# Attention and expert layer on one core: one more row block normalised on VectorE, row ranks and two routing steps placed earlier, and new instruction orders

## The reference

```python
xn = _layernorm(x, axis=-1)
x = x + _L0_attn_ref(xn, Wq, Wk, Wv, Wo) + _L0_ffn_ref(xn, ...)
# attention: 32 query heads of 128 in 8 groups, 8 key heads, causal
q = q * cos + _rotate_half(q) * sin
k = k * cos + _rotate_half(k) * sin
scores = jnp.einsum('bkgtd,bksd->bkgts', qg, k) * scale
attn = jax.nn.softmax(jnp.where(causal, scores, -jnp.inf), axis=-1)
out = jnp.einsum('bkgts,bksd->bkgtd', attn, v)      # then @ Wo.T
# expert layer: 16 experts in 4 groups, best 2 groups, best 2 experts of a row
scores = softmax(xt @ router_w + router_b) + router_bias
y = sum over experts of gate * ((silu(xt @ w1 + b1) * (xt @ w2 + b2)) @ w3 + b3)
z = silu(xt @ sw1 + sb1) * (xt @ sw2 + sb2) @ sw3 + sb3   # shared expert
return (y + z).reshape(shape)
```

## Time and profile before

| | us |
|---|---|
| median of 3 runs | 907.06 (906.69 to 907.95) |
| the profiled execution | 905.59 |
| its span | 903.8 |
| PE busy | 888.5 (98% of the span) |
| DVE busy | 677.7 (75%) |
| ACT busy | 431.2 (48%) |
| POOL busy | 526.5 (58%) |

### The profile page before, as it was taken

How to read it: one execution, slowest core, us unless ns; L and a number is a source line. 1 busy time by engine, 2 the same in 40 slices (tenths; PEclk the granted TensorE clock), 3 DMA queues, 4 the chain that set the end, 5 groups by cost and what they waited for, 6 DMA issues and landing times.

```text
span 903.8 us, 17478 instructions
## 1 busy us (share of the span) xinstructions
PE 888.5 (98%) x5066; PEld 762.2 (84%) x5066; DVE 677.7 (75%) x1614; ACT 431.2 (48%) x1083; POOL 526.5 (58%) x638
## 2 busy tenths in 40 slices
PE   8997999999999999999999999999999999999998
PEld 7786887888888888888888889888888888888886
DVE  6688876687767876768767786768776787676886
ACT  3504543554535644454554545445453564454543
POOL 5923786565654765538554575356565476543663
PEclk9999999999999999999999999999999999999999
DMA  9910223143223532335222443224322252230242
GB/s 329 319 47 15 92 94 123 42 131 121 88 76 86 172 95 79 90 99 168 87 87 76 114 163 87 75 81 126 123 87 75 89 172 94 80 92 22 84 150 94
DMA packets 52161, 97.73 MB, mean 108 GB/s; under 512 B 5920, under 2 KB 17824, under 8 KB 52128
## 3 DMA queue, kind: packets, MB, share of 16 engines
q1 hardware_dynamic: 49568, 88.94, 31.7%
q0 software_dynamic: 2560, 8.39, 2.8%
HBM read 74.76 MB, written 22.54 MB: 108 GB/s over the span
## 4 chain that ended last, share of the span: by engine, by line
PE 92%; DVE 5%; issue 1%; ACT 1%; DMA 0%; POOL 0%; SPq 0%; DVEq 0%
PE bank L1992 10%; PE bank L1990 10%; PE bank L1991 10%; PE bank L2190 7%; PE bank L2129 7%; PE bank L2131 6%; PE bank L2130 6%; PE bank L2226 6%; PE bank L2222 6%; PE bank L2223 6%; PE bank L2206 4%; PE bank L2203 4%; PE bank L2204 4%; PE bank L2251 1%; PE bank L2176 1%
## 5 line engine op out<-in xcount | busy, mean ns | idle before, releaser
L636 POOL TENSOR_SCALAR prob<-prob,rsum 128x128 f32<-128x128 f32 (+3 forms) x256 | 143.9, 582 | 89.8 <-DVE rsum L1480 89.1
L876 ACT ACTIVATE prob<-bank,nmax 128x128 f32<-128x128 f32 (+3 forms) x256 | 133.7, 528 | 113.9 <-DVE nmax L1474 111.3
L1474 DVE CUSTOM_DVE_ANT_0 bank<-bank,causal 128x128 f32<-128x128 f32 (+3 forms) x256 | 122.8, 501 | 35.5 <-PE bank L1992 33.7
L1502 DVE TENSOR_TENSOR pT_lo<-bank,pT_hi 128x512 fp32r<-128x512 f32 x160 | 109.1, 684 | 29.0 <-ACT pT_hi L896 28.6
L896 ACT ACTIVATE pT_hi<-bank 128x512 fp32r<-128x512 f32 x160 | 95.0, 596 | 67.1 <-PE bank L2190 53.4
L2222 PE MATMUL bank<-wo_lo,oT_hi 128*128 128x512 f32 x256 | 106.2, 415 | 0.0
L2129 PE MATMUL bank<-xT_hi,wq_lo 128*128 128x512 f32 x256 | 104.7, 409 | 1.5 <-DVE v_lo L1458 1.4
L619 POOL TENSOR_TENSOR w_lo<-w_raw,w_hi 128x1024 fp32r<-128x1024 f32 x31 | 74.3, 2398 | 52.7 <-ACT w_hi L931 52.7
L2131 PE MATMUL bank<-xT_hi,wq_hi 128*128 128x512 f32 x256 | 101.1, 395 | 0.0
L2226 PE MATMUL bank<-wo_hi,oT_lo 128*128 128x512 f32 x256 | 100.7, 393 | 0.0
L2130 PE MATMUL bank<-xT_lo,wq_hi 128*128 128x512 f32 x256 | 100.6, 393 | 0.0
(11 more groups left out here) (219 smaller groups left out, 2326.5 us busy)
## 6 DMA issues: line engine op xcount, KB each, us to landing
w_raw<-w SPq DMA_DIRECT2D x31, 512.0 KB, 3.5
wq_raw<-wq SPq DMA_DIRECT2D x32, 256.0 KB, 4.1
wo_raw<-wo SPq DMA_DIRECT2D x32, 256.0 KB, 2.8
xg<-x_slots SPq DMA_DIRECT2D x31, 256.0 KB, 3.5
w_raw<-w SPq DMA_DIRECT2D x31, 256.0 KB, 2.8
eb<-b SPq DMA_DIRECT2D x31, 256.0 KB, 3.9
y_slots<-eb SPq DMA_DIRECT2D x31, 256.0 KB, 2.5
x_slots<-pairs SPq DMA_DIRECT2D x3, 2048.0 KB, 16.0
```

What stands on the lines that cost most here:

```text
L636: last = nc.gpsimd.tensor_scalar(row, row, rsum[:, stat(b, i, h)], 1.0, ALU.mult, ALU.mult)
L876: last = nc.scalar.activation(prob[n % 2][:, h, 0:P * (i + 1)], bank[S_BANKS[use % 2]][:, 256 * k:256 * k + P * (i + 1)], ACT.Exp, bias=nm ...
```

## The change

The number of instructions of every kind stays as it is; what changes is where they run and in which order.

- Row block 2 is normalised on DVE, behind blocks 0 and 1, no longer on ACT. POOL's bias additions wait for five blocks of DVE instead of four.
- All four output additions of the first batch come before the group picking on DVE.
- `ranks` is called in the first query projection, after the third of its four blocks of three products, and `count_blocks` and `first_blocks` are called in DVE's prologue, around the first query rotation. `first_places` has three steps left.
- The fifteen tables (five engines by three heads) are in new orders. Among other things, POOL's first scatters stand before `normalise(g, 0, 1)` and SP's loads of `wo` parts 2 and 3 of head 0 stand behind `load_wkv`.

```diff
+        DVE_ROWS, ACT_ROWS = (0, 1, 2, 4, 5), (3, 6, 7)
+
+        def wait_row(engine, n):
+            if n in DVE_ROWS:
+                engine.wait_ge(xn_dve, DVE_ROWS.index(n) + 1)
+            else:
+                engine.wait_ge(xn_act, ACT_ROWS.index(n) + 1)
...
-            pool.wait_ge(xn_dve, 4)
+            pool.wait_ge(xn_dve, len(DVE_ROWS))
...
             def first_head(g):   # GpSimd
+                collect(g, 1)
+                normalise(g, 0, 0)
                 add_k(g, 1, 0)
-                normalise(g, 0, 0)
+                place_x(g, 0)
+                normalise(g, 0, 1)
                 add_q(g, 1, 0)
-                normalise(g, 0, 1)
                 normalise(g, 0, 2)
                 add_k(g, 1, 1)
                 add_q(g, 1, 1)
-                place_x(g, 0)
                 normalise(g, 0, 3)
...
-                for n in (TB * b, TB * b + 1):
+                for n in DVE_ROWS[3 * b:3 * b + 3]:
                     nc.vector.tensor_scalar(xn[:, n, :], y[:, n, :], mv[:, n, 0:1], lnt[:, 2, n:n + 1],
...
             hidden(3)
-            for n in range(2):
+            for n in range(TB):
                 add_down(n)
...
-            for n in range(2, TB):
-                add_down(n)
             spare, one, two = (pick[:, k] for k in range(3))
...
             lo_v(0, 0, 1, FIRST_KV_BANKS[1])
+            count_blocks()
             for h in range(G):
                 turned = first_rot[h % 2]
                 turn_q1(0, 0, h, FIRST_Q_BANKS[h], turned)
                 turn_q2(0, 0, h, FIRST_Q_BANKS[h], turned)
+                if h == 0:
+                    first_blocks()
...
-                    (count_blocks, first_blocks, row_slots, row_gates, experts_of_tiles)[k]()
+                    (row_slots, row_gates, experts_of_tiles)[k]()
...
             def first_head(g):   # VectorE
                 maxima(g, 0, 0, 0)
-                first_places(g, 0)
+                combine_two(g, 1)
                 maxima(g, 0, 0, 1)
                 turn_k(g, 1, 0)
-                first_places(g, 1)
+                inverse_sums(g, 0, 0)
                 lo_v(g, 1, 0)
+                first_places(g, 0)
                 maxima(g, 0, 1, 0)
-                inverse_sums(g, 0, 0)
-                first_places(g, 2)
                 maxima(g, 0, 1, 1)
...
                     project_q(0, 0, h, c, FIRST_Q_BANKS[h])
+                    if (h, c) == (0, 2):
+                        ranks()
...
             def first_head(g):   # TensorE
                 scores(g, 0, 0, 0)
-                first_ranks(g)
                 project_kv(g, 1, 0, 0)
...
             def key_head(g):   # TensorE
+                scores(g, 0, 3, 1)
+                project_out(g, 0, 0, 0)
+                transpose_k(g, 1)
                 scores(g, 0, 3, 2)
                 transpose_p(g, 0, 2, 0)
                 project_out(g, 0, 0, 1)
+                transpose_h(tile_of(g, 1))
                 project_q(g, 1, 2, 0)
```

More of the change, by code:

```diff
@@ new lines, in first_head @@
+                project_q(g, 1, 3, 1)
+                transpose_p(g, 0, 3, 0)
+                project_q(g, 1, 3, 2)
+                project_q(g, 1, 3, 3)
+                transpose_p(g, 0, 3, 1)
+                values(g, 0, 2, 2)
+                project_out(g, 0, 1, 0)
+                project_out(g, 0, 1, 1)
+                project_kv(g + 1, 0, 0, 0)
+                scores(g, 1, 0, 1)
+                values(g, 0, 3, 0)
+                project_kv(g + 1, 0, 0, 1)
+                transpose_p(g, 0, 3, 2)
@@ new lines, in first_head @@
+                transpose_p(g, 0, 3, 3)
+                project_out(g, 0, 1, 2)
+                project_out(g, 0, 1, 3)
+                scores(g, 1, 1, 0)
+                values(g, 0, 3, 1)
+                project_out(g, 0, 2, 0)
+                scores(g, 1, 1, 1)
+                values(g, 0, 3, 2)
+                transpose_p(g, 1, 0, 0)
+                scores(g, 1, 2, 0)
+                values(g, 0, 3, 3)
+                project_out(g, 0, 2, 1)
+                project_q(g + 1, 0, 0, 0)
@@ new lines, in first_head @@
+                project_q(g + 1, 0, 0, 1)
+                project_out(g, 0, 2, 2)
+                project_out(g, 0, 2, 3)
+                project_q(g + 1, 0, 0, 2)
+                scores(g, 1, 2, 1)
+                scores(g, 1, 2, 2)
+                project_out(g, 0, 3, 0)
+                project_q(g + 1, 0, 0, 3)
+                scores(g, 1, 2, 3)
+                transpose_p(g, 1, 1, 0)
+                values(g, 1, 0, 0)
+                project_out(g, 0, 3, 1)
+                project_kv(g + 1, 0, 1, 0)
@@ new lines, in first_head @@
+                project_out(g, 0, 3, 2)
+                project_kv(g + 1, 0, 1, 1)
+                transpose_p(g, 1, 1, 1)
+                project_out(g, 0, 3, 3)
+                scores(g, 1, 3, 0)
+                scores(g, 1, 3, 1)
+                project_q(g + 1, 0, 1, 0)
+                project_q(g + 1, 0, 1, 1)
+                project_q(g + 1, 0, 1, 2)
+                values(g, 1, 1, 0)
+                project_q(g + 1, 0, 1, 3)
+                project_out(g, 1, 0, 0)
+                scores(g, 1, 3, 2)
@@ L2490, in key_head @@
[L2490 to L2492 removed]
+                values(g, 0, 3, 0)
                 project_out(g, 0, 1, 3)
[L2494 to L2497 removed]
+                scores(g, 1, 3, 3)
+                expert_down(tile_of(g, 2))
+                values(g, 0, 3, 1)
                 transpose_p(g, 0, 3, 2)
```

1276 lines of the change are left out of this document (600 added, 676 removed).

## The result

| | before | after |
|---|---|---|
| median, us | 907.23 (906.69 to 907.95, 4 runs) | 917.68 (915.30 to 918.73, 4 runs) |
| ratio, 95% interval | | 1.0111 (1.009 to 1.0132) |
| the profiled execution, its span | 905.59, 903.8 | 917.85, 916.1 |
| PE busy | 888.5 | 895.6 |
| DVE busy | 677.7 | 693.2 |

The forecast was 3.5 us less; it became 10.5 more, outside the range. One figure of the table already points somewhere: DVE has a single instruction more (the row normalisation that it took over from ACT, 0.5 us), yet it is busy 15.5 us longer.

The account below looks back on a forecast made before the run. PE was taken as the bound, with 92% of the chain of waits. Lead -2.0, unexplained pauses -1.0, loop 0 and last head -0.5 made -3.5, from 907.06 to 903.6 us; range 900.8 to 907.0.

Parts of the forecast that it names:

- the key loop: Loop body run six times: keys' low part changes by -0.16 to +0.16 us per head, -1 to +1, taken as 0.
- Rival B: The loop gets a new wait at the key split, 1.1 us each, six times: 909.3 us, slower than before; chance 0.09.
- Start: First rows: one row normalisation moved from ACT to DVE lets PE start near 11.7 us, -0.4 (0.14 to 0.63).
- Additions first: PE's 0.98 us pause at 49.96 us goes, but is given back at the query rotation near 73 us; counted as nothing.
- First blocks in its new place: DVE's 1.1 us call moved between the first and second query rotations, in DVE's idle time; fourth rotation ends at 72.7 us.
- the cover: DVE's idle time around the query rotations, 2.3 us in all, to take in 2.6 us of moved calls.
- The lead of 2.0: Main term: PE's query projection of batch 1 starts at 78.8 instead of 80.82 us; gain 2.0, bounds 0.3 and 2.6.
- The two unexplained pauses: PE waits of 0.65 us at 132.9 and 1.1 us behind DVE's idle before 141.61; 0 to -2.1, taken as -1.0.
- Scatters: POOL's first four scatters go earlier, from about 80.4 to 85.7 us; counted 0, up to +1.3 if they start late.
- Last head: PE's waits for oT and pT splits there, near 2 us in all, shrink: -0.5, bounds -1.5 and +0.8.

Follow-up runs that it names:

- before_new_loop: The kernel before with only the five tables of the repeated key head changed; 919.07 us, ratio 1.0131 to the kernel before.
- loop_before: The changed kernel with the five tables of the repeated key head as before; prologue, first and last head stay changed; 904.38 us, ratio 0.9972.
- adds_back: The changed kernel with repeated and last head tables as before and the third and fourth output addition behind the group picking again; 903.58 us, ratio 0.9987.
- old_tables: The prologue's edits alone, with all fifteen tables as before but for the calls that left them; 904.43 us, ratio 0.9995.
- changed_again: The changed kernel measured once more, on the chip of the last runs; 916.79 us, ratio 1.0131 to the kernel before.
- old_loop_last: The changed kernel with the repeated head's and the last head's tables as before; 902.90 us, ratio 0.9989.
- two_moves: The changed kernel with two DVE calls of the repeated head moved: last_lo_q(g, 0) behind the second maxima, add_out(g, 1, 0) earlier; 906.33 us, ratio 1.0020.
- three_moves: As two_moves, with a third DVE call moved: lo_wo(g, 1) behind lo_kT(g, 1); 912.52 us, ratio 1.0088.
- w3_later: As two_moves, with POOL's small weight split lo_w3(tile_of(g, 1)) behind the query addition add_q(g, 1, 1); 906.94 us, ratio 1.0024.
- filler: As old_loop_last, with 16 unused small transposes on PE between the query projections and the first scores; 902.23 us, ratio 0.9972.
- split_q_later: The changed kernel with one POOL call of the repeated head, split_q(g + 1, 3), moved behind add_q(g + 1, 0, 2); 934.74 us, ratio 1.0338.

## Why the prediction was wrong

The step that failed is the key loop, taken at 0 with -1 to +1. It measured 2.4 us a head, some 14 over six; in whole runs the five tables cost 12.0 (`before_new_loop`) to 13.3 (the changed kernel against `loop_before`). I had worked out how much PE work stands between a key transpose and its product, against a chain of ACT and DVE instructions at the durations they had before. That is right only if their durations don't depend on the order. I had one row that says they do: in the earlier trace rows `q_first` took 0.83 instead of 0.46 us beside a DVE split. I priced that rule at one place, where the moved call was, and did not ask it of the fifteen new tables, where `last_lo_q` had gone from the tenth place of DVE's loop body to the third, into POOL's split of 2.39 us. How far that rule carries: runs that leave DVE's order alone show the port behind the whole pause for the P-split and half of the one for `y`, together 1.1 of the 2.4 us. For the other half of `y` and for `kT_lo` the rows show stretched instructions ahead, and no run shows that these are all of it.

A second term was not in the sum at all: TensorE's clock. I read 1.00 in both stretches and took it to stay. The new prologue left PE two longer pauses near 71 and 73 us, and the clock fell there in twelve of the thirteen traces compared above.

Rival B had the sign, the place (a new wait in the loop, six times) and the rule for its size. It named one wait of the three, the mildest, and a cause (the wide exponential) that the trace does not show: ACT's exponential comes after `kT_hi` there (419.78 and 419.30), and what stands late ahead of it in ACT's queue is an instruction on `both_in` (418.40, after 1.62 us of waiting), which DVE made behind the stretched `wo_lo`. So 909.3 and nine in a hundred were both too low.

Point by point:

- Start: PE's first product came at 11.75 instead of 12.11 us, -0.36 for the -0.4 forecast, and part of that is luck. In the sixteen traces with the new start it lies between 11.51 and 12.73, because the first row normalisation begins anywhere from 8.51 to 9.77. From there to the first product it was 3.21 us in both traces with the old start and 2.96 or 2.97 in fourteen of the sixteen. The edit gives 0.25.

- Additions first: the pause at 49.96 is gone and two others, at 71 and 73 us, have grown from 0.57 and 0.82 to 1.76 and 1.08. Given back, as said, and `adds_back` shows it.

- First blocks in its new place: `per_expert` took 0.84 us where it takes 0.17 alone. The rule that I had let speak and then priced for POOL alone struck DVE here. Those 0.67 us are what the cover that I called "used up nearly whole" did not have: the fourth rotation ended 61.31 us behind PE's first product, where it was 60.79 before. The rows:

```profile
64.11 0.84 DVE L1386 TENSOR_TENSOR per_expert<-per_expert 128x16 f32<-128x16 f32 x1
...
71.11 0.92 PE L2174 MATMUL bank<-k_first,q_first 128*128 128x128 f32 x4 [1.76 <-DVE kT_lo L1467]
73.11 0.58 PE L1993 MATMUL bank<-wkv_hi,xT_lo 128*128 128x256 f32 x1 [1.08 <-DVE prob L1432]
...
80.80 0.50 PE L2127 MATMUL bank<-xT_hi,wq_lo 128*128 128x512 f32 x1 [0.36 <-DVE v_lo L1460]
```

- The lead of 2.0: PE's query projection started at 80.80, not 78.8, as late as before. By the mark I had set, over 80.3, the main term is wrong. The second exponentials did follow the first directly, but PE came to them with two longer pauses and a part of 70 to 80 us at the lower clock. Counted from PE's first product, it is 0.3 us behind before; at a clock of 1.00 it would have been 1.2 ahead (67.49 for 68.71), so the term was too high even without the clock. Near 99 us the lead was small: the key transposes started at 99.89 and 99.75, with 7 more PE instructions begun by then in the changed kernel, an estimated 1 us at 0.12 to 0.23 each.

- The two unexplained pauses: gone, some -1.9 instead of -1.0. They stayed in `before_new_loop` (1.09 and 0.82 us at 133 and 143) and were gone in `old_tables`, which has the old order of the first head. So the prologue's edits remove them, by a way I have not found.

- Together up to 254 us: 2.8 ahead, for -3.0 in the forecast. The sum held by luck: the calls were too high, the pauses too low, and the start came early in this trace; in `changed_again` it is 1.8.

- Scatters: from 83.4 us, not 80.4, to 88.5, and the normalisation behind them at 88.69. No PE pause at 85 to 92 beyond what was there. Costs nothing, as said.

- Last head: about +1 instead of -0.5, by `loop_before` 0.9 over before's 110.4, by `old_loop_last` 1.4. PE waits there for P-splits and, new, for a normalisation on POOL (two of 0.4 and 0.6 us near 898). Wrong in sign.

What stays open: the 0.6 us per head that `two_moves` still has over the old loop; half of the pause for `y`; the third pause (in `three_moves` PE waited for `wo_lo` in its place, in `w3_later` it stayed); and how the pauses at 133 and 143 went. The best ratio is that of `loop_before`, the change without its loop orders, and of `filler`, both 0.28% under before.

## What to carry to other kernels

Before an order is changed in a loop, list the long POOL instructions on SBUF and see which DVE instructions will start inside them; price each such meeting at the rest of the POOL instruction, not at zero (here `q_lo`, 0.55 us alone, ended 0.41 us behind POOL's end). Judge it by durations of one form (shortest, median, longest) and by an engine's busy sum at an equal count of instructions, because this wait is not idle time. Compare the start and the clock over several traces before a tenth of a microsecond is called a hit. A rule worth a sentence at one place of a change is worth asking at every place that the change reorders, the repeated ones first.

## What the runs showed of the hardware

- A DVE split with both inputs in SBUF takes 0.55 us alone and 2.43 beside a POOL split of 2.39 that started 0.37 earlier; a one-tensor `TENSOR_SCALAR` 2.23; a reduction 0.55; a split with one input in PSUM never over 0.69 in 160. The end of the split is 0.40 to 0.42 us behind POOL's end in 24 of 25 cases. POOL is held up as well: `q_first` 0.91 instead of 0.46.

- Four POOL instructions of 256 columns take 3.15 us, one of 1024 takes 2.39, and only the one running holds DVE up.

- In `split_q_later` PE stood still for 2.23 to 2.25 us at six places. Behind four of them its products of 512 columns came 0.43 us apart instead of 0.23 for a while, and the granted clock over 5 us was 0.66; behind the other two (at 266 and 604 us) it stayed at 1.00. So the same pause does not always lower the clock.

- The pauses of 1.76 and 1.08 us at 71 and 73 us (1.29 for the second in most traces) were followed by a granted clock of 0.66 or 0.83 over ten microseconds in twelve traces and of 1.00 in one. With sixteen small transposes in the first pause it was 1.00.
